# A fused attention and mixture-of-experts layer: joined loads of expert groups, router logits from unnormalised rows, idle products in the first wait

## The reference

```python
x = x + xattn(layernorm(x), ctx_512)      # 16 heads over 4096 context rows
x = x + attn(layernorm(x))                # 16 heads, causal, latent q and kv
x = x + ffn(layernorm(x))                 # mixture of 32 experts
```

```python
scores = sigmoid(x @ router_w.T); sc = scores + e_bias
...                                       # best 3 of 8 groups by their top 2, then best 4 experts
topk_w = 2.5 * topk_w / topk_w.sum()
...                                       # each expert takes at most C = 10 tokens
Xp = x[slots_token].reshape(E, C, d)
Y = (silu(Xp @ W_gate) * (Xp @ W_up)) @ W_down
out = scatter(Y * slots_w) + silu(x @ shared_gate.T) * (x @ shared_up.T) @ shared_down.T
```

## Time and profile before

| | |
|---|---|
| median of three runs | 651.63 us |
| profiled execution, its time | 650.6 us |
| its span | 648.7 us |
| busy: TensorE / VectorE / ScalarE / GpSimd | 96% / 58% / 56% / 27% |
| chain that ended last | TensorE 82%, VectorE 6%, issue 4%, ScalarE 3%, DMA 2% |
| DMA | 105.14 MB, 162 GB/s over the span, 398 to 420 GB/s in four of the last five of 40 slices |

### The profile page before, as it was taken

The page is one execution under the profiler, slowest core; times in us unless marked ns, Lnnn a source line. Parts: engine busy times, 40 slices in busy tenths (PEclk is TensorE's granted clock), DMA queues, the critical chain, the costliest instruction groups (busy, mean ns, idle before and its releaser), DMA issues.

```text
span 648.7 us, 15224 instructions
## 1 busy us (share of the span) xinstructions
PE 625.1 (96%) x6035; PEld 466.0 (72%) x6035; DVE 378.8 (58%) x571; ACT 362.0 (56%) x494; POOL 177.7 (27%) x146
## 2 busy tenths in 40 slices
PE   7999999999999999999999999999999999999976
PEld 5986676777777778777777777899556897564443
DVE  5888587866767767767677676655214565501000
ACT  3543665777676677667667676788122874311000
POOL 0270334353453443443444434300000331000000
PEclk7999999999999999999999999999999999999999
DMA  8944884223423422422522521600999107499996
GB/s 338 419 171 94 219 317 98 58 56 74 82 51 65 90 49 59 99 49 51 107 49 43 116 50 36 125 2 3 379 417 371 80 2 250 151 398 411 420 417 224
DMA packets 28648, 105.14 MB, mean 162 GB/s; under 512 B 4288, under 2 KB 8896, under 8 KB 23488
## 3 DMA queue, kind: packets, MB, share of 16 engines
q1 hardware_dynamic: 28608, 104.57, 50.5%
HBM read 77.29 MB, written 0.52 MB: 120 GB/s over the span
## 4 chain that ended last, share of the span: by engine, by line
PE 82%; DVE 6%; issue 4%; ACT 3%; DMA 2%; SPq 2%; POOL 0%; DVEq 0%
PE psO L1128 9%; PE psO L1139 9%; PE psO L1129 8%; PE psS L1115 8%; PE psS L1116 8%; PE psM L1087 5%; PE psO L1207 4%; PE psS L1416 3%; PE psO L1071 3%; PE psS L1050 3%; PE psO L1042 2%; DVE arena L783 2%; SPq L449 2%; PE psO L1073 2%; PE psO L1072 2%
## 5 line engine op out<-in xcount | busy, mean ns | idle before, releaser
L783 DVE TENSOR_REDUCE arena<-psM 128x2 f32<-128x1024 f32 x121 | 147.7, 1221 | 67.4 <-PE psM L1087 67.1
L589 ACT ACTIVATE arena<-psS 128x1024 bf16<-128x1024 f32 x128 | 131.3, 1026 | 87.6 <-PE psS L1116 85.4
L482 POOL TENSOR_TENSOR arena<-arena 128x1024 bf16<-128x1024 f32 x56 | 120.8, 2156 | 190.4 <-ACT arena L591 166.9
L1128 PE MATMUL psO<-arena 128*128 128x129 bf16 x1024 | 132.8, 220 | 0.3 <-DVE arena L801 0.3
L1129 PE MATMUL psO<-arena 128*128 128x128 bf16 x1024 | 132.4, 220 | 0.0
L591 ACT ACTIVATE arena<-psS 128x1024 f32<-128x1024 f32 x129 | 131.0, 1017 | 0.0
L1115 PE MATMUL psS<-arena 128*128 128x256 bf16 x512 | 120.5, 273 | 0.9 <-DVE arena L794 0.9
L1116 PE MATMUL psS<-arena 65*128 65x256 bf16 x512 | 120.8, 273 | 0.0
L1128 PEld LDWEIGHTS psO<-arena 128*128 128x128 bf16 x1024 | 99.1, 98 | 18.8 <-issue 11.2
L1129 PEld LDWEIGHTS psO<-arena 128*128 128x128 bf16 x1024 | 99.4, 97 | 6.7
L822 DVE TENSOR_TENSOR arena<-arena 128x1024 bf16<-128x1024 f32 (+1 forms) x73 | 88.0, 1207 | 15.4 <-ACT arena L591 15.3
(11 more groups left out here) (209 smaller groups left out, 740.5 us busy)
## 6 DMA issues: line engine op xcount, KB each, us to landing
arena<-w_exp SPq DMA_DIRECT2D x27, 1024.0 KB, 19.6
arena<-arena SPq DMA_DIRECT2D x96, 256.0 KB, 3.7
arena<-w_exp SPq DMA_DIRECT2D x31, 512.0 KB, 16.8
arena<-w_pair SPq DMA_DIRECT2D x7, 1088.0 KB, 18.3
arena<-w_exp SPq DMA_DIRECT2D x19, 256.0 KB, 6.0
arena<-w_o SPq DMA_DIRECT2D x1, 4096.0 KB, 18.2
arena<-ctx SPq DMA_DIRECT2D x4, 512.0 KB, 13.1
arena<-rope SPq DMA_DIRECT2D x4, 512.0 KB, 13.9
```

Of the source, the lines that this page charges most:

```text
L482: nc.gpsimd.tensor_tensor(p_lo[:, s % 2, :], p_f[:, s % 2, :], p_hi[:, s % 2, :], ALU.subtract).then_inc(s_plo[0], 1)
L589: nc.scalar.activation(p_hi[:, s % 2, :], psS[s % 2][:, :], ACT.Exp).then_inc(s_phi, 1)
L783: nc.vector.reduce_max(maxes[:, :, st, c], maxima_bank(q, m)[:, :].rearrange("p (j n) -> p j n", j=2), AX.X).then_inc(s_mfree, 1)
L1128: mm(psC[:, st, :], ph, vx[:, GROUP * g + i, 0:CW], start=g == 0 and i == 0 and st == 0, stop=False, skip_group_check=True)
```

## The change

It has three parts.

1. *Loads.* The host stores the experts in the order in which the kernel uses them (k), and one DMA loads a run of them: RUNS lists the runs, 4, 4, 3, 1, 1 for the first 13 places, then four at a time where their places lie side by side, and split where the ring begins anew. So runs are (0-3), (4-7), (8-10), (11), (12), (13-16), (17-20), (21-24), (25), (26-28), (29-31). A group of TensorE waits for every run that holds one of its experts.
2. *Router.* The logits are products of the rows as they are (x, not xn) with centred weights: x.(mean over d of w - w) is minus (x - mean(x)).w, and the scale 1/std of each token goes into the exponential's scale. TensorE sums the router's weights over d (four products, `colsum_mm`) behind the first attention's output projection, and VectorE centres them there. The rows are turned unnormalised, tile by tile as VectorE adds the pieces; the normalised rows are turned after the logits. The exponential is taken tile by tile. Six of the eight products of the shared expert's first part come before the position products and two behind them; `shared_product(0)` moves behind the one-hot rows. Only four of the idle products of this stage stay.
3. *Prologue.* Eight idle products (`WARM_FIRST`) between b0 and a0's wait.

```diff
-WARM_START, WARM_HEADS, WARM_TILE, WARM_LAST, WARM_CHOICE, WARM_ROWS = 9, 3, 2, 3, 3, 4
+WARM_START, WARM_FIRST, WARM_HEADS, WARM_LAST = 9, 8, 3, 4
+SHARED_AHEAD = 6
...
+def refills(g):
+    ks = range(RING + GE * g, min(RING + GE * (g + 1), E))
+    turn = [k for k in ks if k % RING == 0 and k > ks[0]]
+    return [(ks[0], turn[0]), (turn[0], ks[-1] + 1)] if turn else [(ks[0], ks[-1] + 1)]
...
+REFILLS = [refills(g) for g in range((E - RING + GE - 1) // GE)]
+RUNS = [(0, GE), (GE, RING_LOW), (RING_LOW, RING_MID), (RING_MID, RING - 1), (RING - 1, RING)] + [run for group in REFILLS for run in group]
...
-            def load_expert(k, part, done):
-                sp.dma_start(ring[k % RING][:, part], a["w_exp"][expert(k)][:, part]).then_inc(done[k % RING], 16)
+            def load_run(run, part, done):
+                first, end = run
+                o = ring_at[first % RING]
+                places = arena[:, o:o + W_EXP * (end - first)].rearrange("p (k w) -> p k w", w=W_EXP)
+                sp.dma_start(places[:, :, part], a["w_exp"][first:end, :, part].rearrange("k p w -> p k w")).then_inc(done, 16)
...
-            std(3)
+            root(3, 0)
+            for st in range(TT):
+                turned_x(3, st)
+            root(3, 1)
...
-            act.wait_ge(logit_mm, 1)
-            nc.scalar.activation(small[0], psA[0][:, 0:TT * E], ACT.Exp, scale=-1.0).then_inc(sig_exp, 1)
+            for st in range(TT):
+                act.wait_ge(logit_mm, st + 1)
+                act.wait_ge(ln_xn, 2 * (2 * TT + st) + 1)
+                nc.scalar.activation(small[0][:, E * st:E * st + E], psA[st][:, 0:E], ACT.Exp, scale=mv[:, 4 * st + 3:4 * st + 4]).then_inc(sig_exp, 1)
+            for st in range(TT):
+                turned_x(4, st)
             shared_silu(0)
...
+            dve.wait_ge(colsum_mm, 1)
+            nc.vector.scalar_tensor_tensor(w_router, psF[0][:, 0:E].unsqueeze(1).to_broadcast([P, DC, E]), 1.0 / D, w_router,
+                                           ALU.mult, ALU.subtract).then_inc(centred, 1)
...
-            after_tiles(3, x2_mm, 1, x2_banks)
...
+            joined(0, 0)
+            statistics(0, 0)
+            variance(3, 0, 1)
+            joined(1, 0)
+            statistics(1, 0)
+            inverse(0)
+            scaled(0, HALVES[0])
+            joined(1, 1)
+            statistics(1, 1)
+            variance(3, 1, 2)
+            scaled(0, HALVES[1])
+            inverse(1)
+            for half in HALVES:
+                scaled(1, half)
...
                     if n == 0:
+                        warm(WARM_FIRST, psF[1], kt_hi)
                         pe.wait_ge(ld_first_wq, 16)
...
+            for c in range(DC):
+                last = mm(psF[0][:, 0:E], const[:, C_ONES:C_ONES + P], w_router[:, c, :], start=c == 0, stop=c == DC - 1)
+            last.then_inc(colsum_mm, 1)
             pe.wait_ge(ld_wa, 16)
...
                 for j in range(GE):
                     k = GE * g + j
-                    pe.wait_ge(ld_gu[k % RING], gate_up_loaded(k))
+                    if j == 0 or run_of(k) == k:
+                        pe.wait_ge(ld_gu[run_of(k) % RING], gate_up_loaded(run_of(k)))
...
-    arrays["w_exp"] = np.concatenate([np.concatenate(up, 3).transpose(0, 2, 1, 3).reshape(E, P, -1), down], 2)
+    arrays["w_exp"] = np.concatenate([np.concatenate(up, 3).transpose(0, 2, 1, 3).reshape(E, P, -1), down], 2)[[expert(k) for k in range(E)]]
```

More of the change, by code:

```diff
@@ L120, in expert, with run_of, gate_up_loaded, down_loaded @@
     return 12 * trio + each * (k % GE) + r
-def gate_up_loaded(k):
-    pieces = {RING - 1: 2, **{i: DC for i in range(RING, RING + PIECED)}}
-    return 16 * sum(pieces.get(i, 1) for i in range(k % RING, k + 1, RING))
+def refills(g):
[4 more added lines that the diff above has]
+RUNS = [(0, GE), (GE, RING_LOW), (RING_LOW, RING_MID), (RING_MID, RING - 1), (RING - 1, RING)] + [run for group in REFILLS for run in group]
+def run_of(k):
+    return next(first for first, end in RUNS if first <= k < end)
+def gate_up_loaded(first):
+    pieces = {RING - 1: 2, RING: DC}
+    return 16 * sum(pieces.get(f, 1) for f, _ in RUNS if f <= first and f % RING == first % RING)
+def down_loaded(first):
+    return 16 * sum(1 for f, _ in RUNS if f <= first and f % RING == first % RING)
 def wait(eng, sem, value):
@@ L240, in layer @@
         rsum2 = arena[:, w_at + 1856:w_at + 1888].rearrange("p (s h) -> p s h", h=NH2)
-        ring = [arena[:, o:o + W_EXP] for o in [W_EXP * e for e in range(RING_LOW)]
-                + [r_at + W_EXP * e for e in range(RING_MID - RING_LOW)] + [high_at, q_at]]
+        ring_at = [W_EXP * e for e in range(RING_LOW)] + [r_at + W_EXP * e for e in range(RING_MID - RING_LOW)] + [high_at, q_at]
+        ring = [arena[:, o:o + W_EXP] for o in ring_at]
         w_router = cut(DC * E).rearrange("p (c e) -> p c e", c=DC)
@@ L318, in layer @@
         ld_shared = [sem(f"ld_shared{i}") for i in range(2)]
-        ld_gu = [sem(f"ld_gu{i}") for i in range(RING)]
-        ld_down = [sem(f"ld_down{i}") for i in range(RING)]
+        starts = sorted({first % RING for first, _ in RUNS})
+        ld_gu = {i: sem(f"ld_gu{i}") for i in starts}
+        ld_down = {i: sem(f"ld_down{i}") for i in starts}
         ld_end_down = [sem(f"ld_end_down{i}") for i in range(len(END_PARTS))]
@@ L435, in _ @@
             sp.wait_ge(sh_mm, SH_FREES)
-            load_expert(RING - 1, slice(W_GU // 2, W_GU), ld_gu)
-            load_expert(RING - 1, down, ld_down)
+            load_run(held, slice(W_GU // 2, W_GU), ld_gu[RING - 1])
+            load_run(held, down, ld_down[RING - 1])
             load_group(1, down, y_mm, ld_down)
-            last = (E - RING) // GE
+            last = len(REFILLS) - 1
             for g in range(2, last - 1):
@@ L447, in _ @@
             for i, part in enumerate(END_PARTS):
-                for k in new(last):
-                    sp.dma_start(ring[k % RING][:, part], a["w_exp"][expert(k)][:, part]).then_inc(ld_end_down[i], 16)
+                load_run(REFILLS[last][0], part, ld_end_down[i])
             for n in range(2):
```

100 lines of the change are left out of this document (59 added, 41 removed).

## The result

The changed kernel takes **652.64 us** (median of 13 runs, 650.06 to 653.19) and the kernel before, run beside it, 650.07 us (13 runs, 648.61 to 651.67). The ratio is 1.0036 with a 95% interval of 1.0024 to 1.0047: slower by 2.3 us (1.6 to 3.1). Forecast were 648.0 us and "faster"; both are wrong, and the time lies outside the range.

A forecast was written before the change was run, and what follows sets the result against it. The prediction took TensorE's chain (82%) as the bound, and the expert weight stream from about 564 us on. Its terms, -1.8 + 0.8 - 1.9 + 0.1 - 0.8 = -3.6 us, took 651.6 to 648.0 us; range 645.0 to 650.3.

The forecast's parts named there:

- Idle products, -1.8: Prologue: eight idle products hold TensorE's clock up in the first wait, so later work starts earlier: -1.8 us.
- Rival C: Prologue keeps only -0.6 us (clock falls anyway or VectorE gives time back), or router gains -0.9: 649.1 us, chance 0.22.
- Column sums, +0.8: Ahead of the projections: four products summing the router's weights lengthen TensorE's path by 0.8 us.
- Router, -1.9: Router stage: logits from unnormalised rows let the expert weight stream and TensorE behind it start 1.9 us earlier.
- near ties: Router stage: logits hidden behind the table load by 0.1 us, six shared products done 0.15 us before the choice.
- TensorE's path against the stream, +0.1: End: group 6 waits for expert 28, so TensorE's own path ties with the path through the last landing: +0.1 us.
- Stream, -0.8: Expert weight stream: fewer, joined loads raise the rate of the quarter and small last loads: -0.8 us.
- rival B: Quarter and small last loads run at 415 GB/s, so the stream gains -2.6 us: 646.2 us, chance 0.20.
- Rival D: Joined loads stream worse, under 390 GB/s, making the kernel slower; 655.6 us at 380 GB/s, chance 0.08.
- The starting point: Whole kernel: time before the change, taken as the median of three runs, 651.63 us.

The follow-up runs named there:

- c3: Kernel before with the router part alone (column sums included), single expert loads except pairs 14 and 15, 27 and 28: 650.55 us, ratio 1.0007.
- d4: Kernel before with 14 idle products in group 6's wait for its load: 650.48 us, ratio 1.0002.
- c1: Changed kernel with refill runs also cut where a TensorE group begins, all bytes loaded: 649.55 us, ratio 0.9987.
- d1: Kernel before with only the eight idle products in the prologue's first wait added: 651.07 us, ratio 1.0018.
- d2: As c3, but with expert pairs 13 and 14, 26 and 27, so no load crosses two groups: 648.88 us, ratio 0.9989.
- a3: Changed kernel with 24 idle products in group 6's wait, ahead of its gate/up: 650.04 us, ratio 0.9990.
- a1: Changed kernel without the eight idle products of the prologue: 651.34 us, ratio 1.0022.
- a4: Changed kernel with six idle products of 256 columns ahead of each of two further prologue waits: 650.50 us, ratio 1.0000.
- c2: Changed kernel with one load per expert, except pairs 14 and 15, 27 and 28: 651.07 us, ratio 1.0019.
- d3: As c2, but with expert pairs 13 and 14, 26 and 27, so no load crosses two groups: 649.47 us, ratio 1.0000.
- c4: Changed kernel with c1's loads, no prologue idle products, 14 in group 6's wait, column sums moved into a TensorE wait: 647.66 us, ratio 0.9955.
- e1: As e4, plus idle products in the TensorE waits at 66 to 68 us: 647.48 us, ratio 0.9968.
- e2: As c4, but with the column sums where the change has them, ahead of the projections: 648.82 us, ratio 0.9983.
- e3: As c4, but with one load per expert, except pairs 13 and 14, 26 and 27: 648.39 us, ratio 0.9985.
- e4: As c4, with the prologue's eight idle products back and short ones before two further prologue waits, as in a4: 647.06 us, ratio 0.9956.

## Why the prediction was wrong, point by point

**Idle products, -1.8: wrong, and as a single term the largest miss** (+1.37 in the profile). The step that failed reads "From there on TensorE had no wait before 64.6, so the 1.9 us stay". It looked for waits in the kernel before, but an earlier TensorE makes new ones: 0.63 us before a1 and 0.72 us before b2, both of which follow from the step's own times (a1 could start only when ScalarE was done and would end at 19.4, b2 only at 20.0). Behind them the clock was granted at 0.50 for 6 us of fully busy TensorE, where before it had been 0.50 for 10 us with 1.4 us of waits in them. (Two times in the step are off without effect on this: a1 and b2 started at 20.10 and 21.83 before, not at 20.26 and 22.0.) It is not so in every execution: of the seven profiled executions with these products and none for b2, M is at 455.0 to 455.3 in four, 454.07 in one and 452.3 to 452.5 in two; of the eight without the prologue's products, at 453.9 to 454.3 in six and 452.5 to 452.7 in two (c3 and d4, where the clock was back for a part or all of a0, 2.00 and 2.45 us). The forecast -1.8 is about what the two lucky ones with the products show (-1.65 for c1), and lucky ones without them come within 0.4 us of it. On the median of runs d1 measured +1.2 (0.2 to 2.2). Rival C named a fall of the clock all the same, but ahead of q0, where none came, and let it leave -0.6; its floor should have been above zero.

**Column sums, +0.8:** +0.45 in every trace with them (M to X 93.54 to 93.56 against 93.09 to 93.12). The projections behind them start 0.74 us later, where the sum had 0.9 (494.81 against 492.70, less the 1.37 of the prologue), and the turned rows 0.49 later (497.46 against 495.60): the idle time ahead of them gave up 0.25 us, and I had counted it with the 0.17 that the weight load shows. A term that was mis-sized, by 0.35.

**Router, -1.9:** -2.06 in the profile and the same within 0.02 us in every trace with this part. Both near ties held. This part alone, with its column sums, comes to -1.6 by the traces, -0.7 (-1.7 to +0.3) by d2's runs.

**TensorE's path against the stream, +0.1: wrong by 2.5.** The landing (626.3 forecast, 626.1 measured) and the tie were right, as a3 shows. The step that failed is "through the second combination and the products that add x 9.2 as before": these 9.2 us hold group 6's gate/up at 3.64 us, its duration at the clock of before. The wait grew from 3.51 to 6.09 us, the clock fell behind it, the product took 5.92 us, and the path from it to the last down product 19.4 us instead of 17.1, after it had just lost its slack. All kernels that load every byte show together that neither half costs by itself:

| G to E, us | clock falls at group 6 | clock holds |
|---|---|---|
| a load crosses into group 7 | 89.25 to 89.97 (after, a1, a4, c2, c3) | 87.23 (a3) |
| none crosses | 86.66 to 87.57 (c1, d2, d3) | 86.26 to 87.32 (before, c4, d1, d4, e1 to e4) |

c2 and d3, which differ only in which experts share a load, put 2.96 us (89.62 - 86.66) on the crossing where the clock falls in both; a3 puts 2.74 us (89.97 - 87.23) on the fall where there is a crossing in both.

**Stream, -0.8:** nothing in the changed kernel; the stream is as long as before (80.4 us, before 80.3). The step that failed is the third of rival B's gain that was taken without a row behind it: 1 MB loads of 2 KB rows ran at 334 GB/s where 256 KB loads of the same rows had run at 327, so the load count mattered next to nothing, and rival B falls. The rule of the Trainium skill, DMA: Bandwidth & Descriptors, section Rules for kernel authors, to make loads of 1 MiB and more, is not what limits here. That short rows are the limit is not shown either: no kernel changed them.

**Rival D** had the sign, not the cause: no stretch ran under 390 GB/s that had not done so before.

**The starting point** was high by 1.6 us: 651.63 was the median of three runs, 650.07 that of thirteen.

Taken together: the forecast priced every part by durations at the clock of before, and both large misses are products that were met by the lower clock after waits that the change itself made. The miss of 6.0 us in all (+2.4 against -3.6) is 3.2 in the prologue, 3.35 at the end (0.8 of it the stream) and -0.5 in the two other terms.

## What to carry to other kernels

When an engine is made earlier, list the new waits that this creates up to the next point where something else sets the pace; work at half the clock behind them can cost more than was gained. Idle products paid in the last long wait before long work on the critical path (here group 6's: 2.7 us of the changed kernel's G to E for two lines), and cost where they only handed the fall on. When loads are joined, cut them where the consumer waits: a run that holds one expert of the next group made this group wait for it.

## What the runs showed of the hardware beyond that

- Waits of 0.63 and 0.72 us, with TensorE busy for 2.0 us between them (after), and of 1.03 and 0.75 us (d1), were followed by a granted clock of 0.50; 1.31 and 0.71 us (c1) and 1.19 and 0.72 us (d3) were not. At group 6 waits of 3.51 us (before) and 3.07 us (d1) left the clock at 1.00, while 3.14 (c1), 2.91 (d2) and 2.84 us (d3) were followed by a fall. So one trace does not tell whether a wait of this size costs. Why it differs between executions stays open.
- The mean granted clock of an execution goes with its time in the changed kernel: its runs at 0.995 took 650.1 us, those at 0.990 652.0 to 653.2. It is not all. In each of the four comparisons with experiments the runs of before at a mean clock of 1.000 (3, 4, 5 and 4 of them) took 650.1 to 650.2 us on average, and those at 0.995 (9, 4, 5 and 5) 648.8 to 648.9. Why a higher mean clock goes with a longer time there is open.
- Loads of 2 to 4 MB that gather the gate/up parts of several experts, 1.5 MB apart, stream as fast as the single loads of 1 MB did (416 and 417 GB/s from 602 to 636).
